# A second attention whose maximum pass runs half a round earlier, with its projections in other PSUM banks

## The reference, cut to what matters

```python
x = x + attn_a(layernorm(x))          # x: 8 batches, 256 tokens, 128 wide
x = x + ffn(layernorm(x))             # top-1 of 8 experts
x = x + attn_b(layernorm(x))          # the stage of this case
x = x + ffn(layernorm(x))
# attn_b, 16 heads of 8:
q = rope(x @ wq);  lat = x @ w_down;  k = rope(lat @ wk_up);  v = lat @ wv_up
scores = q k^T / sqrt(8), masked by pages of 32 tokens
out = softmax(scores) v;  return out @ wo
```

## Time and profile before

| | |
|---|---|
| runs | 499.72 us median, 498.47 to 499.89 |
| profiled execution | 502.12 us, of it span 500.1 us |
| busy in the span | PE 84%, PE weight loads 65%, DVE 63%, ACT 46%, POOL 43% |
| granted PE clock, mean | 0.905 |
| chain that ended last, by engine | PE 58%, DVE 16%, issue 9%, DMA 6%, ACT 5% |

### The profile page before, as it was taken

How to read it: one execution, slowest core, us unless ns; L and a number is a source line. 1 busy time by engine, 2 the same in 40 slices (tenths; PEclk the granted TensorE clock), 3 DMA queues, 4 the chain that set the end, 5 groups by cost and what they waited for, 6 DMA issues and landing times.

```text
span 500.1 us, 15672 instructions
## 1 busy us (share of the span) xinstructions
PE 419.6 (84%) x5250; PEld 326.9 (65%) x5251; DVE 314.2 (63%) x1173; ACT 232.1 (46%) x565; POOL 214.2 (43%) x312
## 2 busy tenths in 40 slices
PE   8898899998657999986758989989888788799980
PEld 8676588776446999964536556655555566698980
DVE  4765578888744555449576568568876536454543
ACT  2667556666402555301235656756655420255540
POOL 5433335555531344524554635643722433134440
PEclk9989999998757999988788999999998767799996
DMA  8999700000001122130000000000000000111216
GB/s 233 304 242 345 217 3 15 12 11 11 13 17 32 55 65 63 42 90 1 2 2 1 1 1 3 0 0 0 1 2 13 23 17 26 33 49 57 61 47 178
DMA packets 44339, 28.60 MB, mean 57 GB/s; under 512 B 7200, under 2 KB 40480, under 8 KB 44288
## 3 DMA queue, kind: packets, MB, share of 16 engines
q1 hardware_dynamic: 38096, 20.83, 15.0%
q0 software_dynamic: 2496, 5.13, 2.8%
q10 hardware_dynamic: 3696, 1.97, 1.4%
HBM read 12.76 MB, written 15.16 MB: 56 GB/s over the span
## 4 chain that ended last, share of the span: by engine, by line
PE 58%; DVE 16%; issue 9%; DMA 6%; ACT 5%; DVEq 3%; POOL 2%; SPq 1%; another core or an unknown queue 0%; POOLq 0%; ACTq 0%
PE S L1436 7%; PE bank L1446 6%; PE S L1344 6%; PE bank L1303 5%; PE bank L1320 3%; PE bank L1559 3%; DVE nm L757 2%; PE bank L1476 2%; PE S L1276 2%; PE bank L1330 2%; PE bank L1249 2%; PE S L1530 2%; PE bank L1570 2%; PE S L1529 2%; ACT E L1012 2%
## 5 line engine op out<-in xcount | busy, mean ns | idle before, releaser
L916 ACT ACTIVATE E<-S,nmax 128x256 f32<-128x256 f32 x128 | 58.9, 474 | 45.5 <-DVE nmax L541 41.1
L1149 POOL DMA_INDIRECT slots<-yo,token x46 | 44.1, 958 | 73.5 <-DVE yo L697 54.7
L1012 ACT ACTIVATE E<-S 128x1536 f32<-128x1536 f32 x32 | 46.4, 1450 | 24.9 <-PE S L1535 24.8
L1108 POOL TENSOR_TENSOR vs<-Va,rden 128x512 f32<-128x512 f32 x32 | 33.3, 1039 | 57.0 <-DVE rden L576 49.5
L1436 PE MATMUL S<-xgT,W1s 128*128 128x128 f32 x368 | 51.9, 285 | 1.5 <-DVE xgT L683 1.3
L1446 PE MATMUL bank<-W,hT 128*128 x368 | 49.7, 279 | 0.2
L1436 PEld LDWEIGHTS S<-xgT,W1s 128*128 128x128 f32 x368 | 45.3, 194 | 4.5 <-issue 2.1
L973 ACT ACTIVATE hT<-S,b 128x128 f32<-128x128 f32 x92 | 28.7, 363 | 41.8 <-PE S L1436 39.8
L757 DVE TENSOR_REDUCE nm<-bank 128x2 f32<-128x512 f32 x64 | 41.0, 682 | 8.2 <-PE bank L1502 8.1
L1446 PEld LDWEIGHTS bank<-W,hT 128*128 128x128 f32 x368 | 45.6, 195 | 0.5 <-issue 0.5
L541 DVE TENSOR_REDUCE nmax<-S 128x4 f32<-128x1024 f32 x32 | 39.0, 1219 | 10.2 <-PE S L1344 9.4
(11 more groups left out here) (181 smaller groups left out, 984.3 us busy)
## 6 DMA issues: line engine op xcount, KB each, us to landing
rows<-zeros SPq DMA_DIRECT2D x1, 8768.0 KB, 30.8
xg<-rows SPq DMA_DIRECT2D x46, 64.5 KB
W<-in_L_ffn_W SPq DMA_DIRECT2D x1, 2048.0 KB, 10.0
x<-in_L_attn_a_x SPq DMA_DIRECT2D x4, 256.0 KB, 5.7
yg<-slots SPq DMA_DIRECT2D x8, 128.0 KB, 3.5
yg<-slots ACTq DMA_DIRECT2D x8, 128.0 KB, 3.7
slots<-yo,token POOLq DMA_INDIRECT x46
yg<-in_select SPq DMA_DIRECT2D x1, 512.0 KB, 7.8
```

What stands on the lines that cost most here:

```text
L916: last = act.activation(E[:, hp, h, c, :], S[hp % 2][:, h, c * T:(c + 1) * T], ACT.Exp, bias=nmax[:, hp, k:k + 1], accum_out=den[:, hp, k: ...
L1012: act.activation(Eb[:, q % 2, :, :], S4[:, 0:3, :], ACT.Exp, scale=SCALE_B).then_inc(bs["exp"], 1)
L1108: pool.tensor_tensor(vs[:, q, :, :, :], v, r, ALU.mult).then_inc(a_vs, 1)
L1149: pool.indirect_dma_start(out=y_dram, out_offset=bass.IndirectOffsetOnAxis(token[:, turn_at, :], 0), in_=yo[:, turn_at % 2, :], in_offset=None
```

## The change

The pipeline is shifted by half a round for the maximum pass. In round b, PE now makes score groups 2 and 3 of batch b+1 in the first half and groups 0 and 1 of batch b+2 in the second half; DVE takes their maxima in the same order. The rounds start at b = -2. The split of the maxima, their transposes and the copy to mT stand in mid round, before the scores of batch b+2, and mT has two buffers. The projections of batches 2 to 7 no longer use bank 0: `b_q` writes queries to bank 3 and the latent to bank 2, and `b_kv` writes keys to bank 3 and values to bank 2, as four matmuls of 128 columns. Each waits until DVE has drained those banks. `b_q(b+3)` stays in round b; `b_kv(b+2)` comes early in round b, where before `b_kv(b+3)` was in the second half of it. `b_turn_k(b+2)` now leads DVE's round b, and `b_split(b+2)` and `b_repeat(b+2)` stand in the same round, with the first transposes of that batch after them. Half 0 of kT is copied by ACT and half 1 by DVE, the other way round than before. Router steps 1 and 2 go to the end of round 6; the first scatter moves from round 6 to round 7. No computation is added or left out.

The diff, cut to its core ("..." marks lines left out; the rounds' removed lines are in the functions printed above):

```diff
--- before.py
+++ after.py
@@ -175,7 +175,7 @@
-        mT = sb("mT", [P, 2, P], BF16)
+        mT = sb("mT", [P, 2, 2, P], BF16)
@@ -283,7 +283,7 @@
-            for b in (-1, 0):
+            for b in (-2, -1, 0):
-        def router_at(b, point):
-            return {(5, 0): 1, (6, 0): 2, (7, 0): 3, (7, 1): 4, (7, 2): 5, (7, 3): 6, (8, 0): 7}.get(
-                (b, point) if isinstance(b, int) else None)
+        def since(b, first):
+            return not isinstance(b, int) or b >= first
+        def at(b, *rounds):
+            return isinstance(b, int) and b in rounds
+        def proj(b):
+            early = isinstance(b, int) and b < 2
+            return (pb[0], pb[0]) if early else (pb[3], pb[2])
@@ -717,7 +724,8 @@
             def b_turn(b, i, src, done):
-                dve.wait_ge(bs["latT"] if i == 0 else bs["v"], b + 1)
+                if isinstance(b, int) and b < 2:
+                    dve.wait_ge(bs["latT"] if i == 0 else bs["v"], b + 1)
...
                 for u in range(2):
@@ -779,73 +787,77 @@
                 dve.wait_ge(bs["p1"], b + 1)
                 if not isinstance(b, int) or b > 1:
                     dve.wait_ge(bs["split"], b)
...
+                b_turn(b, 0, lambda u: proj(b)[0][:, u * D:(u + 1) * D], bs["turnq"])
             def b_turn_k(b):
                 dve.wait_ge(bs["p2"], b + 1)
...
+                step = 2 if isinstance(b, int) and b < 2 else 1
+                b_turn(b, 1, lambda u: proj(b)[0][:, step * u * D:(step * u + 1) * D], bs["turnk"])
             def b_round(b, p):
...
+                n, m, c, l = there(b + 1), there(b + 2), there(b), there(b - 1)
...
+                if m and since(b, 0): b_turn_k(b + 2)
                 if n: b_kT(b + 1, 1 - p)
...
                 if l: b_normal(b - 1, 0)
...
+                if n: b_max(b + 1, 2)
                 if l: b_normal(b - 1, 1)
...
+                if m and since(b, -1): b_repeat(b + 2, p)
+                if n: b_max(b + 1, 3)
...
                 if l:
                     dve.wait_ge(bs["at"], b)
                     dve.tensor_copy(attT[:, :, :], pb[1][:, 0:T].rearrange("p (u t) -> p u t", u=2)
                                     ).then_inc(bs["attT"], 1)
...
+                if there(b + 3) and since(b, -1): b_turn_q(b + 3)
...
+                if m: b_max(b + 2, 0)
...
                 if l:
                     dve.wait_ge(bs["y"], b)
                     xs = x[:, bass.ds((b - 1) * 2, 2), :]
                     dve.tensor_tensor(xs, xs, pb[1][:, 0:T].rearrange("p (u c) -> p u c", u=2), ALU.add
                                       ).then_inc(bs["x"], 1)
...
+                if m: b_max(b + 2, 1)
...
@@ -987,13 +999,16 @@
-                act.copy(latT[:, :], pb[0][0:LAT, T:2 * T]).then_inc(bs["latT"], 1)
+                act.copy(latT[:, :], proj(b)[1][0:LAT, T:2 * T]).then_inc(bs["latT"], 1)
-                src = pb[0][:, :].rearrange("p (u i h d) -> p u i h d", u=2, i=2, d=DB)
-                act.copy(vst[:, p, :, :].rearrange("p u (h d) -> p u h d", d=DB), src[:, :, 1, :, :]).then_inc(bs["v"], 1)
+                if isinstance(b, int) and b < 2:
+                    src = pb[0][:, :].rearrange("p (u i c) -> p u i c", u=2, i=2)[:, :, 1, :]
+                else:
+                    src = pb[2][:, 0:2 * D].rearrange("p (u c) -> p u c", u=2)
+                act.copy(vst[:, p, :, :], src).then_inc(bs["v"], 1)
@@ -1001,7 +1016,7 @@
-                i = 1
+                i = 0
@@ -1016,35 +1031,34 @@
...
             def b_round(b, p):
...
+                n, m, c, l = there(b + 1), there(b + 2), there(b), there(b - 1)
+                if n: b_qT(b + 1, 1 - p, 1)
                 if l: b_outT(b - 1, 1 - p, 3)
...
+                if m and since(b, 1): b_v(b + 2, p)
                 if c: b_exp(b, 0)
...
+                if at(b, 0): b_v(2, 0)
...
                 if c: b_exp(b, 1)
...
                 if c: b_outT(b, p, 0)
...
+                if m: b_qT(b + 2, p, 0)
                 if c: b_exp(b, 2)
...
+                if there(b + 3) and since(b, -1): b_latent(b + 3)
+                if m: b_kT(b + 2, p)
                 if c: b_outT(b, p, 1)
...
                 if n:
                     act.wait_ge(bs["mt"], b + 2)
...
+                    act.copy(mT[:, 1 - p, :, :], pb[2][:, 0:P].bitcast(BF16).rearrange("p (u t) -> p u t", u=2)
                              ).then_inc(bs["mT"], 1)
...
+                if c: b_exp(b, 3)
...
+                if c: b_outT(b, p, 2)
...
+            def b_router(h):
+                norm_out(3, h - 1, (h - 1) % 2, pb[2])
...
@@ -1200,32 +1214,30 @@
...
             def b_round(b, p):
...
+                if at(b, 5):
                     for c in range(2):
                         inverse_deviation(3, c, c)
+                if there(b + 2) and since(b, -1):
+                    b_split(b + 2, p)
+                if at(b, 5, 6):
+                    inverse_deviation(3, b - 3, (b - 3) % 2)
                 if there(b + 1):
+                    b_maxima(b + 1)
                     b_place_v(b + 1, 1 - p)
...
+                if there(b + 4) and since(b, -1):
                     pool.wait_ge(bs["latT"], b + 3)
                     b_stage(b + 4, p)
...
+                if at(b, 7):
+                    inverse_deviation(3, 4, 0)
                     scatter(1, 0, 0)
...
                     scatter(1, 1, 1)
                     inverse_deviation(3, 5, 1)
                     for c in (2, 3):
                         scatter(1, c, c % 2)
                     inverse_deviation(3, 6, 0)
                     scatter(1, 4, 0)
...
+                if at(b, 8):
                     inverse_deviation(3, 7, 1)
                     scatter(1, 5, 1)
@@ -1457,16 +1469,26 @@
                     pe.wait_ge(norm[2]["xnT"], b + 1)
                 else:
                     pe.wait_ge(bs["xb"], b - 1)
+                if not isinstance(b, int) or b > 1:
+                    pe.wait_ge(bs["max"], ((b - 2) * 4 + 3) * 3 + 2)
+                to_q, to_lat = proj(b)
                 for u in range(2):
-                    pe.matmul(pb[0][:, u * D:(u + 1) * D], xb[:, p, u * P:(u + 1) * P], wq[:, :], start=True, stop=True)
-                pe.matmul(pb[0][0:LAT, T:2 * T], wdown[:, :], xb[:, p, :], start=True, stop=True).then_inc(bs["p1"], 1)
+                    pe.matmul(to_q[:, u * D:(u + 1) * D], xb[:, p, u * P:(u + 1) * P], wq[:, :], start=True, stop=True)
+                pe.matmul(to_lat[0:LAT, T:2 * T], wdown[:, :], xb[:, p, :], start=True, stop=True).then_inc(bs["p1"], 1)
             def b_kv(b):
                 pe.wait_ge(bs["latT"], b + 1)
-                pe.wait_ge(bs["turnq"], b + 1)
-                for u in range(2):
-                    last = pe.matmul(pb[0][:, 2 * u * D:2 * (u + 1) * D], latT[:, u * P:(u + 1) * P], wkv[:, :],
-                                     start=True, stop=True)
+                if isinstance(b, int) and b < 2:
+                    pe.wait_ge(bs["turnq"], b + 1)
+                    for u in range(2):
+                        last = pe.matmul(pb[0][:, 2 * u * D:2 * (u + 1) * D], latT[:, u * P:(u + 1) * P], wkv[:, :],
+                                         start=True, stop=True)
+                else:
+                    pe.wait_ge(bs["max"], ((b - 1) * 4 + 1) * 3 + 2)
+                    for i, bank in enumerate(proj(b)):
+                        for u in range(2):
+                            last = pe.matmul(bank[:, u * D:(u + 1) * D], latT[:, u * P:(u + 1) * P],
+                                             wkv[:, i * D:(i + 1) * D], start=True, stop=True)
                 last.then_inc(bs["p2"], 1)
...
@@ -1572,91 +1594,93 @@
             def b_round(b, p):
...
+                n, m, c, l = there(b + 1), there(b + 2), there(b), there(b - 1)
+                if at(b, -2):
+                    pe.wait_ge(bs["turnk"], 2)
+                    pe.wait_ge(bs["v"], 2)
+                if n: b_tq(b + 1, 1 - p, 1)
+                if m and since(b, 1): b_kv(b + 2)
+                if l:
+                    pe.wait_ge(bs["ot"], b * 4 - 1)
+                    b_values(b - 1, 1 - p, 3)
...
+                if c: b_scoresT(b, p, 0)
+                if at(b, 0):
+                    b_scores(1, 1, 1)
+                    b_kv(2)
...
+                if n: b_tk(b + 1, 1 - p, 1)
+                if l: b_natural(b - 1, 1 - p, 0)
                 if n:
...
+                    if m:
                         pe.wait_ge(bs["turnk"], b + 3)
                         pe.wait_ge(bs["v"], b + 3)
...
+                    b_scores(b + 1, 1 - p, 2)
+                if c: b_scoresT(b, p, 1)
...
                 if l:
...
+                    pe.wait_ge(bs["att"], b * 2 - 1)
                     b_natural(b - 1, 1 - p, 1)
...
+                if n: b_scores(b + 1, 1 - p, 3)
...
                 if c:
                     if l: pe.wait_ge(bs["att"], b * 2)
...
+                    b_values(b, p, 0)
...
+                if m: b_tq(b + 2, p, 0)
```

(66 more changed lines are left out.)

158 lines of the change are left out of this document (41 added, 117 removed).

## The result

The changed kernel takes 531.67 us (median of 4 runs, 527.44 to 533.57) against 499.81 (4 runs): ratio 1.061, 95% interval 1.053 to 1.070. It is slower, as forecast, but by 31.9 us and not by 17.8, and outside the range. Some executions of a kernel take a few per cent longer at a lower clock, so every ratio here compares the fast runs of a kernel with the fast runs of before that were timed beside it; a median is that of all its runs.

The account below looks back on a forecast made before the run. PE was taken to bound the stage (16.14 of 17.48 us a round). Loop 8.4, head 6.7, rounds 5 and 6 0.5 and clock 2.2 sum to 17.8 on 502.1: 519.9, less 2.4 for the median, 517.5 us; range 508 to 526.

Parts of the forecast that it names:

- the chain: Loop: projection, rotation, split, repeat and first transposes of batch b+2 all in round b; +2.1 us a round, +8.4 in all.
- the split's end: Loop round: POOL's 6.65 us split, begun at 3.0 us behind the rotation, ends at 9.65 us.
- the query transposes: Loop round: transposes of batch b+2 start at 10.6 us, after 8.2 us of PE work, so PE idles 2.4 us.
- The wait for mT: Loop, second half of the round: PE waits 1.0 us for ACT's late mT copy before the next scores.
- Keys and values: Projection as four 128-column matmuls: 1.20 us instead of 0.99, +0.2 us a round.
- The sum of the steps: Loop: the round's steps and waits added up give 19.6 us, against 17.5 before.
- one stretch of low clock: Round 0: after 3.5 idle us the clock falls to 0.50 and the PE work behind takes twice as long, +2.2 us.
- The head: Start through round 0: waits for maxima and the split chain cost +6.7 us, or 8.9 with round 0's clock.
- what follows the loop: Rounds 5 and 6: 19.6 us and near 16, against 34.8 for both before; together +0.5 us.
- the missing queries: Round 5: their absence is made up by two last-norm steps ahead of the split on POOL; round stays 19.6 us.
- The faster case: Rival: the split chain ends before PE reaches the transposes and waits are filled; 8 us gained, 491.7 us; chance 0.08.
- The rival with the clock: Rival: idle 2.4 us a round brings clock 0.50 in four more rounds, 2.2 us each; 526.3 us; chance 0.15.

Follow-up runs that it names:

- idle_filled: Changed kernel plus four unused 256-column matmuls into bank 0 before the query transposes in rounds 0 to 5: 525.46 us, ratio 1.047.
- all_idle_filled: Changed kernel plus unused matmuls before the query transposes in rounds 0 to 5 and at PE's waits in rounds -2 to 0: 515.05 us, ratio 1.040.
- round5_reordered: mT_first_head_filled with round 5's last-norm steps put behind the rotation on DVE and behind the key split on POOL: 500.15 us, ratio 1.008.
- mT_copy_first: Changed kernel with queries split a round ahead on POOL and ACT's mT copy put before its copy out of bank 1: 508.08 us, ratio 1.027.
- mT_first_head_filled: mT_copy_first plus unused 256-column matmuls into bank 1 wherever PE waited in rounds -2, -1 and at the start of 0: 502.2 us, ratio 1.013.

## Why the forecast was right in kind and wrong in size

**Right.** The bound, the sign, and in the loop the chain and its length. From the round's first transposes (the loop's second round, 310.33) the forecast had the split's end at 9.65 us; it came at 9.66 (319.99 - 310.33). It had the query transposes at 10.6; they came at 11.0 there (10.8 on average), since DVE's repeat begins 0.55 us behind POOL's last operation and not 0.15. The wait for mT was put at 1.0 us and is 0.7. Keys and values were taken at 1.20 us and take 1.08 (310.89 to 311.97), between the old form's 0.99 and the forecast. By the Trainium skill's figure (TensorE: Matmul & The Clock Gate, "Wait — 56ns, not 53.3ns?"), 2.5 ns for each matmul beside its columns, splitting the columns is nearly free; the trace is nearer to that (0.09 us more) than to the forecast's 0.2. The sum of the steps, 19.6 us, is what idle_filled shows at the full clock.

**The step that failed is the clock in the loop.** The forecast booked one stretch of low clock, 2.2 us in round 0, and gave its fall in the loop 0.15, on the ground that PE stays over 80% busy. PE is busy for 84% of these rounds (72.04 of 85.50) and the clock falls in each of them, behind the gap of 2.0 to 2.3 us. A share over a whole round says nothing of the stretch in which the gap lies. This is 1.8 us a round: 7.1 in the loop, and idle_filled takes 6.9 off the stage in all. From A to D the forecast lacked 13.2 us (17.8 against 31.0), and the 7.0 that it lacked in the loop are these. The Trainium skill (TensorE: Matmul & The Clock Gate, "HAM oscillation — how this bites in real kernels") describes this pattern, a gap in each turn of a loop and a slow clock behind it, there for a longer gap that waits for a DMA; this trace agrees, with a gap of 2.3 us and 0.51 from 322 to 325 us.

**The head and the rounds from 5 on were too small as well.** The head lost 11.9 us and not 8.9. Round 0 is not the cause: it took 24.1 us (265.35 to 289.40), where the forecast with its clock term had 24.5. Rounds -2 and -1 took 20.7 us, where it had 17.2. The clock was low in them, too (0.63 over the stretch), but with the fills of all_idle_filled and a clock of 0.92 they still took 20.5. What the forecast missed there stays open. For what follows the loop it had +0.5 (its own terms, 19.6 and 16 against 34.8, make 0.8), and 3.7 were lost. Round 5 took 20.3 us instead of 19.6. The forecast let the missing queries pay for the norm's steps, but the steps stand ahead of the split and the queries behind it, and round5_reordered gains by moving them, on a kernel with a shorter split. The other 2.5 us lie in rounds 6 to 8 and are no more than what one kernel differs by there from profile to profile. The forecast took its 0.3% for the smallest difference that can be told; the intervals measured here are 0.4% to 1.4% to either side.

**The rivals.** The faster case was far off: the split chain decides, as the forecast's condition for it said. The rival with the clock was the true one. It put 8.8 us on the loop, where 7.1 were measured, and even its 526.3 lacked the head and what follows the loop. The range should have included it with room above.

## What to carry to other kernels

When a producer chain is moved nearer to its consumer, add up the chain in its new place against the work that stands between, before asking what the move frees; here 10.6 us against 8.2 decided it. And when the sum leaves PE a gap of 2 us in every round, price the clock in every round, not once: here a gap of 2.0 to 2.3 us cost 1.8 us more behind it. Cheap useless matmuls in such a gap tell the two apart in one run.

## What the runs showed of the hardware

The granted clock fell to about 0.50 behind a gap of 2.0 to 2.3 us in each of the four loop rounds of after, though PE was busy for 84% of them, and was back at 1.00 in the same round. With 1.99 us of useless work in the gap it stayed at 1.00 for 96 us. The same code can go either way: round 5 ran at 1.00 in mT_copy_first and at 0.91 in mT_first_head_filled.

DVE's repeat started 0.55 us after POOL's last operation of the split, on a semaphore that an instruction of its own raises; DVE's rotation started 0.03 us behind the end of PE's projections (312.05 to 312.08, an end that is modelled).
